# Attention and mixture-of-experts block on one core: residual additions moved to GpSimd at the end, and another order for the last loads

## The reference

```python
x = x + _layernorm(attention(_layernorm(x)))
x = x + _layernorm(moe(_layernorm(x)))
# moe: shared(xf) + sum over e of expert_e(xf) * gate[:, e]
# _layernorm(y): (y - mean(y)) / sqrt(var(y) + 1e-5), over the 128 numbers of a token
```

## Time and profile before

| what | value |
|---|---|
| median of 3 runs | 384.76 us (382.99 to 386.19) |
| the profiled execution: its own time | 383.89 us |
| its span, first to last instruction | 382.0 us |
| granted TensorE clock, mean over the span | 0.958 |
| busy share: PE, DVE, ACT, POOL | 88%, 76%, 67%, 74% |

### The profile page before, as it was taken

One profiled execution on the slowest core, in us unless ns is written; L12 is line 12 of the kernel. 1 busy time (PEld: TensorE's weight loads), 2 busy tenths in 40 slices (PEclk: granted clock), 3 DMA queues, 4 the chain that ended last, 5 costly groups with the idle time before them and its releaser, 6 DMA issues.

```text
span 382.0 us, 8164 instructions
## 1 busy us (share of the span) xinstructions
PE 336.9 (88%) x2497; PEld 292.0 (76%) x2497; DVE 289.2 (76%) x688; ACT 256.6 (67%) x692; POOL 284.4 (74%) x381
## 2 busy tenths in 40 slices
PE   7879797998999998989898995958999999989991
PEld 2538485796886868768598894948999999989971
DVE  4999999799999899999936663524554459787667
ACT  4949864887986978767246764216556666688764
POOL 8877898578788787888768888874666767866640
PEclk9969996999999999999999999886999999999997
DMA  6576767575473406143188387945788879988317
GB/s 194 166 218 168 174 180 123 115 207 133 145 194 104 140 29 199 36 135 101 33 257 259 113 226 204 243 149 159 217 263 257 251 242 367 350 246 263 125 52 205
DMA packets 53522, 69.18 MB, mean 181 GB/s; under 512 B 6365, under 2 KB 37386, under 8 KB 53482
## 3 DMA queue, kind: packets, MB, share of 16 engines
q1 hardware_dynamic: 47556, 58.58, 53.9%
q0 software_dynamic: 4544, 9.35, 7.2%
q10 hardware_dynamic: 1382, 0.79, 0.8%
HBM read 40.06 MB, written 18.15 MB: 152 GB/s over the span
## 4 chain that ended last, share of the span: by engine, by line
PE 39%; DVE 17%; ACT 11%; POOL 11%; issue 10%; another core or an unknown queue 6%; SPq 2%; DMA 2%; DVEq 0%; ACTq 0%; POOLq 0%
PE bS L1550 7%; PE bO L1550 7%; PE bO L1334 6%; DVE KV L1701 3%; ACT hs L1024 2%; DVE KV L1692 2%; POOL expert_lists L707 2%; DVE SH L2071 2%; PE bV L1523 2%; POOL Z L789 2%; PE bV L1525 2%; PE bV L1524 2%; DVE w_lo L2124 1%; POOL Z L794 1%
## 5 line engine op out<-in xcount | busy, mean ns | idle before, releaser
L830 POOL DMA_INDIRECT expert_results<-yb,yrow x78 | 77.5, 994 | 39.5 <-issue 19.2
L707 POOL DMA_INDIRECT expert_lists<-rows,pos x64 | 64.3, 1004 | 19.7 <-issue 17.7
L1701 DVE TENSOR_TENSOR_SCAN KV<-bS,KV 128x1024 f32<-128x1024 bf16 x32 | 72.8, 2277 | 0.6 <-POOL KV L733 0.3
L1334 PEld LDWEIGHTS bO<-wout_rot,Z 128*128 128x128 f32 x512 | 60.5, 192 | 8.1 <-POOL Z L789 4.5
L1334 PE MATMUL bO<-wout_rot,Z 128*128 128x128 f32 x512 | 63.0, 277 | 1.9 <-POOL Z L789 1.1
L2148 DVE COPY yrow<-xb 128x2 int32<-128x2 int32 x24 | 6.8, 284 | 47.0 <-PE bS L1550 17.0
L1153 ACT ACTIVATE hs<-bV,KV 128x256 f32<-128x256 f32 x56 | 21.9, 474 | 21.1 <-remote 10.0
L1550 PE MATMUL bO<-KV,hs 128*128 128x128 f32 x232 | 29.2, 276 | 2.9 <-ACT hs L1153 1.9
L1550 PEld LDWEIGHTS bO<-KV,hs 128*128 128x128 f32 x232 | 27.5, 192 | 3.6 <-ACT hs L1153 3.4
L1304 PE MATMUL bA<-w2s_sb,hs 128*128 128x128 f32 x224 | 28.8, 277 | 0.0
L1523 PE MATMUL bV<-x_lo,w_hi 128*128 128x256 f32 x80 | 24.4, 305 | 4.2 <-DVE x_lo L2127 3.5
(11 more groups left out here) (370 smaller groups left out, 997.4 us busy)
## 6 DMA issues: line engine op xcount, KB each, us to landing
KV<-packed_weights SPq DMA_DIRECT2D x21, 578.0 KB
Z<-packed_weights SPq DMA_DIRECT2D x18, 578.0 KB
xb<-expert_lists SPq DMA_DIRECT2D x39, 129.0 KB
vr<-vr SPq DMA_DIRECT2D x16, 224.0 KB, 2.5
shared<-expert_results SPq DMA_DIRECT2D x7, 512.0 KB
vr<-vr SPq DMA_DIRECT2D x16, 192.0 KB
vr<-vr SPq DMA_DIRECT2D x16, 160.0 KB
vr<-vr SPq DMA_DIRECT2D x16, 128.0 KB
```

The source lines that it names most:

```text
L707: g.indirect_dma_start(out=lists, out_offset=bass.IndirectOffsetOnAxis(ap=pos[:, m:m + 1], axis=0), in_=rows[:, m // TILES, m % TILES, :], ...
L830: g.indirect_dma_start(out=results, out_offset=bass.IndirectOffsetOnAxis(ap=yrow[n][:, c], axis=0), in_=yb[n][:, c, :], in_offset=None).th ...
L1334: ins = t.matmul(bO[:, j * D:(j + 1) * D], Z[:, d, j * P:(j + 1) * P], wout_rot[:, d], start=False, stop=True, skip_group_check=True)
L1701: v.tensor_tensor_scan(w, ps_keep, w, 0.0, ALU.mult, ALU.add).then_inc(s["kv_sum"], 1)
```

## The change

GpSimd makes the residual additions of groups 6, 4 and 5 (in this order) after its last scatter, with its own semaphore `fin_rest`, and VectorE no longer makes them. SyncE's three stores of these groups wait for `fin_rest`, and the counts of `fin_last` for the last two stores fall by three. The four loads of group 7 are issued for tiles 2, 3, 0, 1 and no longer for 0, 1, 2, 3.

```diff
-            for j in range(TILES):
+            for j in [*range(ON_PE, TILES), *range(ON_PE)]:
...
-            store(sp, 6, "fin_last", 5)
-            store(sp, 4, "fin_last", 6)
-            store(sp, 5, "fin_last", 7)
+            store(sp, 6, "fin_rest", 1)
+            store(sp, 4, "fin_rest", 2)
+            store(sp, 5, "fin_rest", 3)
             for half in range(2):
                 n = NT - TILES + 2 * half
-                sp.wait_ge(s["fin_last"], 8 + half)
+                sp.wait_ge(s["fin_last"], 5 + half)
...
             each_block(step)
+            def rest(group):
+                at = slice(TILES * group, TILES * (group + 1))
+                g.tensor_tensor(SH[:, at], SH[:, at], X[:, at], ALU.add).then_inc(s["fin_rest"], 1)
+            pool.wait_ge(s["fin_own"], 3)
+            rest(6)
+            pool.wait_ge(s["fin_n"], 5)
+            rest(4)
+            pool.wait_ge(s["fin_n"], 6)
+            rest(5)
...
             scaled(6, lambda j: SH[:, TILES * 6 + j], range(TILES))
-            dve.wait_ge(s["fin_own"], 3)
-            residual(6)
-            normed(4)
-
             late_gated()
             final_mean(7, lambda j: late_y[j])
-            normed(5)
             dve.wait_ge(s["fin_root"], 2)
```

More of the change, by code:

```diff
@@ L298, in sandwich_kernel @@
             tab_done tab_turned gate_exp gate_w fin_gate fin_sum fin_st fin_mv fin_pow fin_shift fin_n
-            fin_root fin_own fin_half fin_last out_stored""".split()
+            fin_root fin_own fin_half fin_last fin_rest out_stored""".split()
         s = {n: sem(n) for n in names}
```

## The result

| | before | changed |
|---|---|---|
| median | 383.05 us (6 runs, 381.58 to 386.19) | 387.61 us (6 runs, 386.10 to 388.92) |
| profiled execution, its span | 383.89, 382.0 us | 388.92, 387.2 us |

The ratio of changed to before is 1.012 with a 95% interval of 1.0088 to 1.0153: slower by 4.6 us, where 0.8 us faster was forecast, outside the range given (382.3 to 385.7).

A forecast was written before the change was run, and what follows sets the result against it. VectorE's work after the last loads was taken to bound the end. Terms of -1.24 us and +0.44 us for the shift sum to -0.80 us, giving 384.0 us from the median, range 382.3 to 385.7.

The forecast's parts named there:

- Two additions leave the front, -1.25.: On VectorE, gated sums of tiles 2 and 3 begin at 373.45, not 374.70, helped by the load order: -1.25 us.
- TensorE's tiles are late, +0.15.: Tile 1 lands at 374.5, so VectorE waits for TensorE before tile 0's statistics: +0.15 us, bounds 0 and +0.6.
- The third addition leaves, -0.14, sum -1.24.: VectorE's reciprocal follows the root without a third addition between: -0.14 us; the shift would start at 376.76, not 378.00.
- GpSimd's additions, 373.5 to 377.2: GpSimd's three additions start at 373.5, 374.7 and 375.9 and end at 377.2, from products of 1.27 us each.
- The rival of slow additions: GpSimd's additions become the bound: -0.5 us at 1.5 us each, 0 at 1.7; time 384.3 to 384.8, chance 0.17.
- the slower case: Late third addition delays stores ahead of group 7's halves in SyncE's queue: +2.0 us at 2.36 each, 386.8; chance 0.06.
- The shift stands for GpSimd, +0.44.: VectorE's shift, with two SBUF inputs, due at 376.76, stands until GpSimd's third addition ends at 377.2: +0.44 us.
- SyncE and the DMA engines, 0.: Stores of groups 6, 4 and 5 move to about 374.8, 376.0 and 377.2, ahead of group 7's first half: 0.
- The 1.89 us outside the span and the time after the last data are not touched.: At the kernel's end, both stretches were taken as unchanged by the edit, adding nothing to the forecast.
- the end hangs on VectorE: In the last stretch VectorE works without a hole from 373.44, and its work was taken to set the end.
- the chain: Profile view of the chain that ended last: which engine's work leads to the kernel's end.
- within 1%: Outcome "same", chance 0.94: a measured change under 1%, which is 3.8 us, more than any case considered.

The follow-up runs named there:

- the small kernel: A separate kernel copying only 512 rows, with 0 to 142 awaited indirect DMAs and a memset on GpSimd; DRAIN 166 ns for 0, 9180 for 110, 2563 for 142.

## Why the prediction was wrong

Its steps, against the trace of the changed kernel (times from the issue of the last loads at 370.81, and at 370.15 before):

- *Two additions leave the front, -1.25.* Right, and a little more: the gated sums begin right behind the normalizing of group 6, with no wait for a load, 3.18 us after the loads and not 4.55, which is -1.37. The run with the old order shows the waits (0.51 and 0.31 us) that the new one takes away; of these only 0.43 us reached the store, as with the old order the wait for TensorE and the long shift went too.
- *TensorE's tiles are late, +0.15.* Right: a wait of 0.18 us. Tile 0's statistics begin 1.97 us after the sums and not 1.71, +0.26 with this wait in it.
- *The third addition leaves, -0.14, sum -1.24.* Right: the shift begins at 6.64 us, before at 7.85: -1.21.
- *GpSimd's additions, 373.5 to 377.2, which is 3.35 to 7.05.* Right: 3.35 to 7.06, 1.24 us each. The rival of slow additions fell here, and with it the slower case, whose mechanism (a late third addition before the stores) did not occur.
- *The shift stands for GpSimd, +0.44.* The mechanism was right and the price a little high: 0.44 us long and not 0.16, so +0.28, and it ended with the third addition, at 377.89 and 377.87. It is what the earlier trace rows show, where a VectorE instruction with two SBUF inputs, begun 0.13 us behind one of GpSimd's, took 1.69 us and not 0.68, and what the run where GpSimd added group 6 shows in its addition of 1.21 us and not 0.68. That the gated sums stay free beside GpSimd was right as well: their four took 1.26 us, as before.
- *SyncE and the DMA engines, 0.* Right: the first half was stored 0.93 us sooner, and SyncE, with its stores landed, was at the end 381.4 - 370.81 = 10.6 us after the loads and not 11.6.
- *"The 1.89 us outside the span and the time after the last data are not touched."* The second half of this sentence is the step that failed, and with it the sentence that the end hangs on VectorE. Outside the span little changed (388.92 - 387.2 = 1.7 us), but the time after the last data, from 381.4 to the end of the span, was 0.6 us before and is 5.8 us in the changed kernel. The forecast followed the chain to the last store and took what came behind for constant. It read who waits for GpSimd's additions (the stores), and not that the closing barrier waits for GpSimd itself. GpSimd's DRAIN was in the trace of before, 11.6 us long at line 79, with 3.9 us to spare; the busy counts leave such instructions out (POOL is 0.00 from 381.2 to 387.0 in the changed kernel, while its DRAIN runs), and none of the rows behind the forecast shows that line. Moving GpSimd's end from 368.77 to 377.87, 8.4 us later against the loads, used up the 3.9 us and 4.5 more; the medians differ by 4.6.

No rival held it. One of them also had a step wrong: with additions of 1.5 us the third would run from 376.5 to 378.0, so that the shift, due at 376.76, would by the same full stop stand to 378.0 and not to 376.8, and nothing of the gain would be left where -0.5 us was put; no run had such additions. The chance of 0.94 for "within 1%" rested on the argument that no case reached 3.8 us, and the list of cases was not complete.

## What to carry to other kernels

Before work is put on an engine that is idle at the end, look at that engine's own closing instructions in the trace and at how much later the program may reach them: free time before its end is not free when the end itself is long. On GpSimd in this kernel, with its 142 indirect DMAs, this was 9.1 us; everything given to it had to be done 9.1 us before the last store landed. The DMAs had all been waited for by semaphores, and opening the block without that DRAIN took the limit away (ratio 0.9978 and not 1.012). No run tried this with an indirect DMA that nobody had waited for.

A wait at a closing barrier that is put down to an engine long done is not to be believed (here TensorE, done at 376.0, for a barrier passed at 387.0): the rows of the barrier's own line show who came last.

## What the runs showed of the hardware

- GpSimd's DRAIN goes on after all its DMAs have landed (by 370.81 in the changed kernel, where it ran from 376.3 to 386.9): in the small kernel 82 ns for each indirect DMA issued, 9.2 us for 110, starting anew at 113 (1.2 us for 125), with a pause of 1.6 us ahead of the 114th. In the whole kernel with 142 it was done 9.1 us after GpSimd's last work or last wait in every trace with this DRAIN (377.8 for 368.77 before, 386.9 for 377.87 in the changed kernel), and the same 9.1 with 148; there the count of 113 does not hold.
- It is the duration of the instruction: with a bare wait ahead of it and 10 us of idle time it still took 9.06 us.
- A VectorE instruction of four columns with two SBUF inputs stood until GpSimd's addition had ended (0.44 and 0.50 us long in two kernels, 0.16 where no addition ran; in the run with six more indirect DMAs 0.72, from 382.54 to 383.26, with GpSimd's addition over at 383.23), and one of 512 columns took 1.21 us and not 0.68. VectorE's gated sums and statistics, with one input in PSUM or one in all, ran beside GpSimd's additions at their old times: 1.26 us for the four sums in both kernels, 0.49 and 0.50 for the statistics, two by two, where it was 0.50 and 0.48, and 0.38 for the four variances in both.
